# Two graph layers on one core: the setup of the first layer's node powers, reordered

## The reference

```
h = relu(layernorm(x));  x = x + L0(h, adj)
h = relu(layernorm(x));  x = x + L1(h, adj, adj)

L0:  h = x @ fc_w.T + fc_b;  x0 = x
     alph = sigmoid(alpha)[:, None];  w_eff = w * clip(d, 0, 1) @ w.T
     8 times:  h = h + (alph * 0.5 * (adj @ h - h) + h @ w_eff - h + x0) / 8
L1:  lam = largest eigenvalue of L;  Ln = 2 L / lam - I
     h = relu(layernorm(Ln @ x @ Wc + bc) * g1 + be1);  x1 = h + x
     attention of 4 heads, masked by adj > 0, out @ Wo + bo, layernorm (g2, be2)
     MLP with gelu, layernorm (g3, be3)
```

## Time and profile before

| | us |
|---|---|
| median of 3 runs | 911.24 (910.99 to 911.51) |
| profiled execution | 910.41 |
| its span, first to last instruction | 908.5 |

### The profile page before, as it was taken

How to read it: one execution, slowest core, us unless ns; L and a number is a source line. 1 busy time by engine, 2 the same in 40 slices (tenths; PEclk the granted TensorE clock), 3 DMA queues, 4 the chain that set the end, 5 groups by cost and what they waited for, 6 DMA issues and landing times.

```text
span 908.5 us, 19047 instructions
## 1 busy us (share of the span) xinstructions
PE 862.2 (95%) x6765; PEld 705.9 (78%) x6765; DVE 652.3 (72%) x2110; ACT 541.3 (60%) x1234; POOL 327.1 (36%) x426
## 2 busy tenths in 40 slices
PE   6999999999999999987999999999999999999993
PEld 5779999998989888975777777767777777667883
DVE  6855564645453546535889888899898888987996
ACT  3134343434243233225888888888888888886884
POOL 4111111111111212301445545555455454424886
PEclk9799999999999999999999999999999999999997
DMA  3000000000000000402445555444445554420122
GB/s 102 0 12 13 12 12 13 12 13 13 13 12 13 12 24 1 124 16 76 121 102 122 140 140 141 125 109 110 101 117 141 140 140 127 109 46 2 48 70 70
DMA packets 46428, 61.73 MB, mean 68 GB/s; under 512 B 3567, under 2 KB 21246, under 8 KB 46334
## 3 DMA queue, kind: packets, MB, share of 16 engines
q1 hardware_dynamic: 46034, 60.38, 26.0%
q10 hardware_dynamic: 300, 0.13, 0.1%
HBM read 39.53 MB, written 20.97 MB: 67 GB/s over the span
## 4 chain that ended last, share of the span: by engine, by line
PE 44%; DVE 3%; ACT 2%; issue 2%; DMA 1%; POOL 0%; SPq 0%; DVEq 0%; ACTq 0%; POOLq 0%
PE bank L1769 13%; PE bank L1789 8%; PE bank L1756 6%; PE bank L1831 4%; PE bank L1509 3%; PE bank L1491 2%; PE bank L359 2%; PE bank L1838 1%; PE bank L268 1%; PE bank L368 1%; PE bank L363 1%; DVE prob L1938 1%; PE bank L1472 1%; ACT prob L1881 1%; DMA q_stack<-bounce_k 1%
## 5 line engine op out<-in xcount | busy, mean ns | idle before, releaser
L1881 ACT ACTIVATE prob<-prob,low 128x512 f32<-128x512 f32 x256 | 183.9, 720 | 22.3 <-DVE low L1938 22.1
L1938 DVE CUSTOM_DVE_ANT_0 prob<-bank,mask 128x512 f32<-128x512 f32 x256 | 171.8, 686 | 20.1 <-PE bank L1756 18.5
L1769 PE MATMUL bank<-ident,prob 128*128 128x128 f32 x1024 | 160.8, 280 | 0.0
L1769 PEld LDWEIGHTS bank<-ident,prob 128*128 128x128 f32 x1024 | 115.0, 141 | 40.9 <-issue 24.5
L1864 ACT ACTIVATE probT<-bank 128x512 f32<-128x512 f32 x176 | 104.8, 595 | 39.7 <-PE bank L1769 38.7
L1756 PE MATMUL bank<-k_stack,q_stack 128*128 128x512 f32 x256 | 122.8, 480 | 4.8 <-DVE low L1938 3.3
L820 PE MATMUL bank<-B_hi,halves 128*128 128x384 f32 x384 | 107.4, 342 | 1.6 <-DVE halves L1183 1.1
L791 PE MATMUL bank<-halves,P3T_hi 128*128 128x256 f32 x512 | 95.4, 288 | 3.4 <-DVE halves L1201 2.2
L610 POOL TENSOR_SCALAR var_eps<-mv 128x4 f32<-128x4 f32 x16 | 3.6, 226 | 243.8 <-DVE mv L1127 243.8
L791 PEld LDWEIGHTS bank<-halves,P3T_hi 128*128 128x128 f32 x512 | 81.7, 194 | 5.8 <-DVE halves L1201 2.5
L1789 PE MATMUL bank<-probT,v 128*32 128x128 f32 x2048 | 82.2, 279 | 0.2 <-DVE probT L1925 0.2
(11 more groups left out here) (265 smaller groups left out, 1960.5 us busy)
## 6 DMA issues: line engine op xcount, KB each, us to landing
k_stack<-bounce_q SPq DMA_DIRECT2D x64, 256.0 KB, 5.0
q_stack<-bounce_k SPq DMA_DIRECT2D x64, 256.0 KB, 7.4
bounce_q<-k_parts SPq DMA_DIRECT2D x16, 512.0 KB, 2.8
bounce_k<-q_parts SPq DMA_DIRECT2D x16, 512.0 KB, 3.1
x_in<-in_x_dram SPq DMA_DIRECT2D x16, 256.0 KB, 2.8
out_dram<-probT SPq DMA_DIRECT2D x16, 256.0 KB, 2.3
y<-in_adj_dram SPq DMA_DIRECT2D x4, 256.0 KB, 3.7
W1s<-in_L_gnn_W_dram SPq DMA_DIRECT2D x1, 128.0 KB, 2.2
```

What stands on the lines that cost most here:

```text
L1769: last = pe.transpose(psum[2 + u % 2][:, mt * P:(mt + 1) * P], prob[u % RING][:, mt * P:(mt + 1) * P], ident[:, :])
L1881: act.activation(prob[u % RING][:, :], prob[u % RING][:, :], ACT.Exp, bias=low[:, u % TURNED:u % TURNED + 1], scale=-1.0, accum_out=row_su ...
L1938: dve.tensor_tensor_reduce(prob[u % RING][:, :], psum[u % 2][:, :], mask[:, u // HEADS, :], 1.0, 3e38, ALU.add, ALU.min, low[:, u % TURNED ...
```

## The change

Four edits, all in the setup.

- The nine rows of the second layer are loaded straight into `bc_all`, each broadcast to 128 partitions by its load. `row_in`, the matmuls with ones (L733) and the copies (L1165) go. `z_out` and `norm_z` of batch 0 wait for the loads.
- U becomes 0, 1 and the row sum of Pn, and is split in halves by VectorE. TensorE multiplies the halves with those of PT: 12 matmuls with three weight columns and 512 moving columns give three rows of 512 in bank 6. VectorE adds a one to the first row and has `U_rows`, in the setup. L723, GpSimd's sum PT and the transposes of U (L744) go.
- The second power runs in three passes over all four banks, one for each product of halves. The pass with Pn's low parts is last and alone waits for them.
- The high parts of Pn are made two by ScalarE and two by VectorE. VectorE's sum S is moved behind the powers of W and the low parts of PT.

```diff
@@ loads (SyncE)
-                        sp.dma_start(one.row_in[:, n, :], row.rearrange("(o d) -> o d", o=1)
+                        sp.dma_start(one.bc_all[:, n, :], row.rearrange("(o d) -> o d", o=1).broadcast_to([P, D])
                                      ).then_inc(one.rows_loaded, 16)
@@ GpSimd
                 for mt in range(NT):
-                    pool.wait_ge(Pn_hi_ready, mt + 1)
+                    if mt < NT // 2:
+                        pool.wait_ge(Pn_hi_ready, mt + 1)
+                    else:
+                        pool.wait_ge(P_ready, 2 * NT + mt - NT // 2 + 1)
...
-                pool.wait_ge(PT_lo_ready, NT)
-                pool.tensor_tensor(out=PT[:, :, :], in0=PT_parts[0][:, :, :].bitcast(F32),
-                                   in1=PT_parts[1][:, :, :].bitcast(F32), op=ALU.add).then_inc(PT_sum_ready, 1)
@@ TensorE
-                pe.wait_ge(Pn_lo_ready, NT)
-                pe.wait_ge(PT_lo_ready, NT)
-                for mt in range(NT):
-                    node_power(mt, PT_parts, P2_psum)
+                pe.wait_ge(Pn_hi_ready, NT // 2)
+                pe.wait_ge(P_ready, 2 * NT + NT // 2)
+                pe.wait_ge(PT_hi_ready, NT)
+                for n, (left, right) in enumerate(products(Pn_parts, PT_parts)):
+                    for mt in range(NT):
+                        if n == 0:
+                            pe.wait_ge(PT_lo_ready, mt + 1)
+                        if n == 2 and mt == 0:
+                            pe.wait_ge(Pn_lo_ready, NT)
+                        for k in range(NT):
+                            last = pe.matmul(psum[mt][:, :], left[:, k, mt * P:(mt + 1) * P], right[:, k, :],
+                                             start=n == 0 and k == 0, stop=n == 2 and k == NT - 1)
+                        if n == 2:
+                            last.then_inc(P2_psum, 1)
...
-                pe.wait_ge(PT_sum_ready, 1)
-                pe.wait_ge(U_ready, 2)
-                for nt in range(NT):
-                    for k in range(NT):
-                        last = pe.matmul(psum[6][:, nt:nt + 1], PT[:, k, nt * P:(nt + 1) * P], U[:, k, 1:2],
-                                         start=k == 0, stop=k == NT - 1)
+                pe.wait_ge(U_ready, GROUP + 2)
+                for k in range(NT):
+                    for n, (u, p) in enumerate(products(U_parts, PT_parts)):
+                        last = pe.matmul(psum[6][0:GROUP, :], u[:, k, :], p[:, k, :], start=k == 0 and n == 0,
+                                         stop=k == NT - 1 and n == 2)
                 last.then_inc(setup_psum, 1)
                 pe.wait_ge(B_step, STEPS + 1)
-                pe.wait_ge(one.rows_loaded, 16 * ROWS)
-                row_flat = one.row_in[:, :, :].rearrange("o r d -> o (r d)")
-                for c in range(3):
-                    if c == 2:
-                        pe.wait_ge(U_ready, GROUP)
-                    cols = min(N, ROWS * D - c * N)
-                    pe.matmul(psum[4 + c][:, 0:cols], ones[0:1, :], row_flat[:, c * N:c * N + cols], start=True,
-                              stop=True).then_inc(one.rows_spread, 1)
...
-                    for nt in range(NT):
-                        pe.transpose(psum[1][0:GROUP, nt * P:(nt + 1) * P], U[:, nt, :], ident[:, :])
...
-                pe.wait_ge(one.rows_copied, 3)
+                pe.wait_ge(rows_ready, 1)
@@ ScalarE
-                for mt in range(NT):
+                for mt in range(NT // 2):
                     act.wait_ge(P_ready, NT + mt + 1)
                     act.activation(Pn_parts[0][:, mt, :], Pn[:, mt, :], ACT.Copy).then_inc(Pn_hi_ready, 1)
@@ VectorE
+                dve.wait_ge(P_ready, 2 * NT)
+                for t in range(NT // 2, NT):
+                    dve.tensor_copy(Pn_parts[0][:, t, :], Pn[:, t, :]).then_inc(P_ready, 1)
                 power_out(4)
-                dve.wait_ge(adjT_ready, NT)
-                dve.tensor_tensor(out=S[:, :, :], in0=A[:, :, :], in1=adjT[:, :, :], op=ALU.add).then_inc(S_ready, 1)
...
                 turned_lo(NT - 1, PT_parts, NT)
-                dve.memset(U[:, :, 0:1], 1.0).then_inc(U_ready, 1)
+                dve.memset(U[:, :, 0:1], 0.0).then_inc(U_ready, 1)
+                dve.memset(U[:, :, 1:2], 1.0).then_inc(U_ready, 1)
+                dve.wait_ge(adjT_ready, NT)
+                dve.tensor_tensor(out=S[:, :, :], in0=A[:, :, :], in1=adjT[:, :, :], op=ALU.add).then_inc(S_ready, 1)
...
-                dve.tensor_reduce(U[:, :, 1], Pn[:, :, :], AX.X, ALU.add).then_inc(U_ready, 1)
+                dve.tensor_reduce(U[:, :, 2], Pn[:, :, :], AX.X, ALU.add).then_inc(U_ready, 1)
+                dve.wait_ge(U_ready, GROUP)
+                dve.tensor_copy(U_parts[0][:, :, :], U[:, :, :]).then_inc(U_ready, 1)
+                dve.wait_ge(U_ready, GROUP + 1)
+                dve.tensor_tensor(out=U_parts[1][:, :, :], in0=U[:, :, :], in1=U_parts[0][:, :, :].bitcast(F32),
+                                  op=ALU.subtract).then_inc(U_ready, 1)
...
                 dve.wait_ge(setup_psum, second_U)
-                dve.tensor_copy(U[:, :, 2], psum[6][:, 0:NT]).then_inc(U_ready, 1)
-                for c in range(3):
...
+                dve.tensor_scalar(U_rows[:, :], psum[6][0:GROUP, :], ident[0:GROUP, 0:1], None,
+                                  ALU.add).then_inc(rows_ready, 1)
```

More of the change, by code:

```diff
@@ L132, in two_layers @@
         one = Shared()
-        one.row_in = tensor(whole, "row_in", [1, ROWS, D])
         one.bc_all = tensor(whole, "bc_all", [P, ROWS, D])
@@ L178, in two_layers @@
         one.mlp_loaded = sem("mlp_loaded")
-        one.rows_spread = sem("rows_spread")
-        one.rows_copied = sem("rows_copied")
         one.stats_ready = sem("a_stats")
@@ L276, in z_out @@
     at_least(dve, one.z_std_ready, b)
+    if b == 0:
+        dve.wait_ge(one.rows_loaded, 16 * ROWS)
     dve.tensor_tensor(out=one.z[:, :, :], in0=bank[:, :].rearrange("p (t d) -> p t d", d=D),
@@ L326, in norm_z @@
     pool.wait_ge(one.z_std_ready, b + 1)
+    if b == 0:
+        pool.wait_ge(one.rows_loaded, 16 * ROWS)
     pool.tensor_tensor(out=one.z_gain[:, :, :], in0=one.z_std[:, :, :], in1=all_tiles(one, G1),
@@ L445, in layer0 @@
         U = sb("U", [P, NT, GROUP])
+        U_parts = [sb(f"U_{part}", [P, NT, GROUP], F32R) for part in ("hi", "lo")]
         beta = sb("beta", [P, STEPS + 1])
@@ L485, in layer0 @@
         C2 = sb("C2", [P, NT, D])
-        A, Pn, PT = (y[:, i * NT * N:(i + 1) * NT * N].rearrange("p (t n) -> p t n", n=N) for i in range(3))
+        A, Pn = (y[:, i * NT * N:(i + 1) * NT * N].rearrange("p (t n) -> p t n", n=N) for i in range(2))
         PT_parts, P2T_parts, P3T_parts = (tuple(sb(f"{n}_{part}", [P, NT, N], F32R) for part in ("hi", "lo"))
@@ L501, in layer0 @@
         PT_psum = sem("PT_psum")
-        PT_sum_ready = sem("PT_sum_ready")
         setup_psum = sem("setup_psum")
@@ L1393, in bias_rows_out @@
                     dve.wait_ge(setup_psum, bias_turned)
-                    dve.tensor_copy(U_rows[:, :], psum[1][0:GROUP, :]).then_inc(rows_ready, 1)
                     dve.tensor_copy(beta_rows[:, :], psum[2][0:GROUP, 0:GROUP * D]).then_inc(rows_ready, 1)
```

## The result

| | before | changed |
|---|---|---|
| median us (4 runs each) | 911.12 (910.59 to 911.51) | 904.37 (903.25 to 905.86) |
| profiled execution, span | 910.41, 908.5 | 903.38, 901.5 |
| TensorE busy | 862.2 | 853.2 |

The ratio is 0.9927, 95% interval 0.9908 to 0.9946: 6.7 us faster. Forecast were 5.0 us and 906.2, range 903.6 to 908.6. The four executions took 903.3, 903.4, 905.4 and 905.9 us; the profiled one is among the two short ones.

What follows compares the result with a forecast made beforehand. TensorE, nearly always busy after 64 us, was taken as the bound, so setup gains count one for one. First squaring from 56.92 to 51.9 gains 5.0: 910.41 less 5.0 is 905.4, plus 0.8 gives 906.2; range 903.6 to 908.6.

Steps and rivals of the forecast that it cites:

- the slow start of the third power: Forecast case, chance 0.45: third power begins at 1.2 GHz and loses 1.6 us; first squaring at 51.9, gain 5.0.
- a slow stretch disappears: Rival, chance 0.13: the half-clock stretch at 64.70 to 68.10 goes, worth 1.7 us more; 904.2 us.
- Setup before the bound: TensorE is almost always busy after 64 us, so setup time gained ahead of its main stream counts one for one.
- the mark: TensorE's first squaring, at 56.92 us before; from there its instructions are the same in both kernels; predicted at 51.9.
- Start: Up to the second power: two copies replace S in VectorE's queue; second power at 18.79, 1.24 us earlier.
- Three passes: Second power: bank 0 completes later, VectorE idles 1.0 us, its low part starts at 27.9, third power at 35.6.
- Pause: TensorE idles 2.8 us ahead of the third power, from 32.8 to 35.6, where it had worked.
- Signs of being wrong: Wrong if second power after 19.5, first adj transpose after 7.3, or first squaring moves by 5 and the end doesn't.
- Routes to the mark: From 35.6 to the first squaring: VectorE's chain reaches it at 51.35, TensorE's at 50.4 full clock or 52.5 slow.
- the case that was given 0.17: Rival, chance 0.17: VectorE decides up to the first squaring, clock full; gain 5.5 us, 905.7 us.
- the full-clock case: Third power at full clock, VectorE deciding the first squaring at 51.35; gain 5.5 us, chance 0.17.
- Loads: Rival, chance 0.06: row loads push adj back by 2.35 us, 908.6, or half, 907.4; otherwise they cost nothing.

Runs made afterwards that it cites:

- after_again: The changed kernel, unaltered, measured and profiled once more beside other runs on another chip; 904.09 us, ratio 0.9915 to the kernel before.
- a_rowsfirst: The changed kernel with the nine broadcast row loads issued ahead of the loads of adj; 911.74 us in one run.
- a_warm: The changed kernel with ten unused matmuls of ones by ones while TensorE waits for the first loads; 903.04 us, ratio 0.9904 to the kernel before.
- a_oldsums: The changed kernel with the old row sums back (32 one-column matmuls, GpSimd's sum PT, transposes of U); 906.12 us, ratio 0.9943 to the kernel before.
- b_rows: The kernel before with only the broadcast row loads, without the matmuls with ones and the copies; 906.87 us, ratio 0.9961.
- b_power: The kernel before with the second power in three passes, two high parts on VectorE and S moved later; 912.34 us, ratio 1.0012.
- b_order: The kernel before with two high parts on VectorE and S moved later, the second power in one pass behind all low-part waits; 908.12 us, ratio 0.9977.
- b_sums: The kernel before with only the new row sums (12 products of halves), rows still spread by TensorE; 905.15 us, ratio 0.9941.
- a_onepass: The changed kernel with the second power in one pass over the banks, all low-part waits ahead of it; 905.21 us, ratio 0.9929 to the kernel before.
- a_mask: The changed kernel with VectorE's mask moved behind the third power, into the first pair; 904.42 us, ratio 0.9922 to the kernel before.
- a_best: The changed kernel with one-pass second power, mask in the first pair, Sq written in one step, ScalarE's P2T high part earlier; 902.95 us, ratio 0.9900 to before.
- a_bestwarm: a_best with ten unused matmuls of ones by ones ahead of the loads; 900.66 us, ratio 0.9885 to the kernel before.

## Why the prediction was right

The time fell inside the range, and the sums up to the start of the third power held to 0.4 us. The case on which the forecast rested, the slow start of the third power, is not what the profiled execution shows, so part of the agreement is luck: 904.37 lies next to the 904.2 of the rival "a slow stretch disappears", but the stretch is there, at 57.7, and the time comes from other terms.

- **Setup before the bound.** "What is gained ahead of TensorE's main stream counts one for one": right. From the mark to 357 us the lead goes from 6.1 to 6.8 us, at the end it is 7.0.
- **Start.** Second power 18.47, predicted 18.79. The two casts take 0.37 each, not 0.42, and their cost is nothing: they fit between two powers, whose copies go on every 0.87 us. The low parts on GpSimd ended at 18.26 instead of 19.94, because S no longer runs beside the first of them (4.97 us for four, 6.62); S now starts beside the last and takes 2.96 instead of 2.28. In both kernels the one that started second lost about what was left of the first: GpSimd 1.6 us where S had 1.7 to go, S 0.7 where GpSimd had 0.8.
- **Three passes.** VectorE's first low part of P2T: predicted 27.9, measured 27.56, with 0.37 us of waiting instead of 1.0. Third power: predicted 35.6, measured 35.51.
- **Pause.** Predicted 2.8 us, measured 3.0.
- **Signs of being wrong.** Two were set too tight. The second power was to start by 19.5: it did here, at 18.47, but came at 20.20 in after_again, at a time inside the range. The first adj transpose was to come by 7.3: it came at 7.33, and at 7.36 in the kernel before.
- **Routes to the mark.** VectorE's 51.35 predicted, 50.84 measured. That is the case that was given 0.17. TensorE's route with the slow start was the forecast (0.45), and did not happen in this execution; it did in after_again and a_rowsfirst, and with 3.4 us of low clock in a_warm. As a forecast of one execution the step "it begins at 1.2 GHz and loses 1.6 us" failed, as a statement on the kernel it holds in three of the four traces that have its pause of 3.0 us (changed, after_again, a_warm, a_rowsfirst). Its size was right in a_warm (third power 12.6 us, 1.6 more than 11.0) and too small in after_again and a_rowsfirst (13.8 in both, 2.8 more), beyond the 2.15 that were taken as the most. What it missed is that in these three traces, and in a_oldsums, no slow stretch follows in the first pair, so that the totals differ by less than the marks. In before, b_rows, b_power and b_order both came. What decides between the two is not shown.
- **Small slips in the sums.** The gain of the full-clock case is 56.92 - 51.35 = 5.57, not 5.5. The four transposes of U took 0.44 us before (56.24 to 56.68), not 0.33. Neither changes a case.
- **The 2 us that were missing.** The spans differ by 7.0 us, not 5.0: 1.1 at the mark (0.6 the clock, 0.5 the smaller terms above) and 0.9 behind it, which no step had. Of these 0.7 come evenly between 70 and 357 us: 1362 matmuls take 0.5 us less, 0.35 ns each in the mean. The same stretch of the stream by window, before and changed:

```profile
69.50:300.00 230.50, 230.50 (x1362) 212.22 (x1360) 117.25 (x411) 85.07 (x188) 30.12 (x52) 1.00 0.04 12
63.38:293.40 230.02, 230.02 (x1362) 211.68 (x1360) 117.70 (x413) 85.14 (x188) 30.37 (x52) 1.00 0.04 12
```

This pace is in every kernel that allocates the two small tensors U_parts (0.6 to 0.7 us gained between 70 and 290 us), a_oldsums included, which doesn't multiply by them, and in none of b_rows, b_power and b_order, which don't allocate them (0.0). That points to the addresses of the tensors allocated behind them; no run changed the addresses alone, so it is not shown.
- **Loads.** They don't push adj back: first adj transpose 7.33 against 7.36. But "a load of 64 KB lands in 2.2 us" was wrong for them, and the rival's price of 2.35 us for all of them ahead of adj was too small by a factor of four (9.3 us in a_rowsfirst).

From the list of DMA issues of the changed kernel (KB each, median us to landing), four of the nine rows, and a weight issued behind them that lands late too:

```profile
bc_all<-in_L_gnn_be_dram SPq DMA_DIRECT2D x3, 64.0 KB, 9.0
bc_all<-in_L_gnn_b_dram SPq DMA_DIRECT2D x1, 64.0 KB, 10.1
W_c<-in_L_gnn_Wc_dram SPq DMA_DIRECT2D x1, 64.0 KB, 9.4
```

Before, W_c landed in 2.2 us.

## What to carry to other kernels

Thin matmuls can cost twice: their own time, and the clock of what follows. In all five traces with the one-column matmuls ahead of the third power the clock was low in it (before, b_rows, b_power, b_order, a_oldsums), in none of the five without them and with a pause of at most 2.2 us (b_sums, a_onepass, a_mask, a_best, a_bestwarm), and in three of the four with a pause of 3.0 us. So look for what lowers the clock ahead of a long product before counting instructions. When a setup passes between engines, compute both routes to a common mark, since two edits on one route don't add up once the other decides. And look at marks and distances in the traces beside the times, in more than one trace of a program where they are to settle a microsecond: executions of one program lay 2 to 7 us apart here, as much as any one of these edits.

## What was not expected of the hardware

- Nine loads in a row that each broadcast one row of 512 B to 128 partitions landed 5.5 to 10.1 us after issue, behind adj and x, where a plain 64 KB load took 2.2. Much of that is waiting for each other: with nothing ahead the first took 3.8 us, and they landed 1.2 us apart. Ahead of adj they delay it by 9.3 us.
- Matmuls with three weight columns, 512 moving columns and all 128 rows kept the clock at 1.00 in the two kernels that had only them ahead of the third power without a long pause (a_best, a_bestwarm); with a pause of 3.0 us behind them it stayed up in one of four profiles (changed, but not after_again, a_warm, a_rowsfirst), with no edit to tell the one from the other. The pauses of 2.2 and 1.8 us in a_onepass and a_mask left it up, and so did the 2.57 us of one-partition matmuls in b_sums.
- At the start of the program the clock isn't up, whatever the column of the window says (1.00 from the start): groups of four transposes took 1.06 us until between 10 and 16 us into the execution (19 in a_rowsfirst, where adj comes late), and 0.60 behind. With ten matmuls in the dead time ahead of the loads all groups took 0.60 (a_warm, a_bestwarm).
